# Four-stage MetaFormer: attention keys as the normed tokens, last tile centred by matmul, another late order, upper convolution rows by diagonal matmuls

## What is computed

```python
# stage 0, mixer: depthwise 3x3 convolution over 64 channels per image
xv, z = split(norm(x) @ in_proj_w.T)
xc = silu(depthwise_conv3x3(xv, conv_w, 'SAME') + conv_b)
# stage 2, feed-forward: 1024 serial steps over the pixels, 2 batches
yt = sigmoid(wx_t + yt @ V.T)
# stage 3, mixer; xn = (x - mean) / sqrt(var + eps) over the 32 channels
q, k, v = xn @ Wq, xn @ Wk, xn @ Wv          # 32 channels = 4 groups of 8, 2 heads of 4
# group 0: inside 8x8 windows, group 1: across them; group 2: inside 16x16, group 3: across
sim = einsum('id,jd->ij', q * 4 ** -0.5 ..., k) + pos   # the scale is DIM_HEAD ** -0.5
out = softmax(sim) @ v
x = x + concat(out_0..out_3) @ Wo + bo
```

## Time and profile before

| | us |
|---|---|
| median of 3 runs (lowest, highest) | 1099.59 (1097.26, 1099.84) |
| the profiled execution, its own time | 1096.21 |
| its span | 1094.3 |
| TensorE matmul busy | 735.8 (67%) |
| VectorE busy | 447.8 (41%) |
| ScalarE busy | 447.1 (41%) |
| POOL busy | 256.5 (23%) |
| recurrence's matmuls L835, 2048 records | 269.4 |
| its sigmoids L847, 1024 | 165.0 |

### The profile page before, as it was taken

The page is one execution under the profiler, slowest core; times in us unless marked ns, Lnnn a source line. Parts: engine busy times, 40 slices in busy tenths (PEclk is TensorE's granted clock), DMA queues, the critical chain, the costliest instruction groups (busy, mean ns, idle before and its releaser), DMA issues. The chain is left out here.

```text
span 1094.3 us, 11753 instructions
## 1 busy us (share of the span) xinstructions
PE 735.8 (67%) x4391; PEld 412.7 (38%) x4391; DVE 447.8 (41%) x746; ACT 447.1 (41%) x1473; POOL 256.5 (23%) x143
## 2 busy tenths in 40 slices
PE   7917888887886787655555555557887555685876
PEld 3302333333343443333333333334654333353543
DVE  5597999999956555400000000021152000220753
ACT  4454767676625543233333333332222333223532
POOL 3267989898810000200000000000000000000410
PEclk9966999999996588655555555555555555555887
DMA  3020000000000000200000000000000000000000
GB/s 67 2 58 0 1 0 1 0 1 0 1 1 5 1 22 9 63 1 1 1 1 0 1 1 1 1 1 0 1 1 1 1 1 0 1 1 1 1 22 11
DMA packets 9474, 7.64 MB, mean 7 GB/s; under 512 B 7154, under 2 KB 7970, under 8 KB 9128
## 3 DMA queue, kind: packets, MB, share of 16 engines
q1 hardware_dynamic: 9416, 6.88, 2.6%
HBM read 5.04 MB, written 0.26 MB: 5 GB/s over the span
## 5 line engine op out<-in xcount | busy, mean ns | idle before, releaser
L835 PE MATMUL L2p_z<-L2yx,L2v 64*32 64x2 f32 x2048 | 269.4, 199 | 230.5 <-ACT L2yx L847 225.5
L847 ACT ACTIVATE L2yx<-L2p_z 32x2 f32<-32x2 f32 x1024 | 165.0, 161 | 387.5 <-PE L2p_z L835 387.5
L835 PEld LDWEIGHTS L2p_z<-L2yx,L2v 64*32 64x32 f32 x2048 | 181.6, 136 | 336.3 <-ACT L2yx L847 316.6
L1486 DVE COPY xn<-L2yx 32x512 f32<-32x512 f32 (+2 forms) x3 | 1.0, 328 | 389.0 <-ACT L2yx L847 361.8
L621 POOL TENSOR_TENSOR hc<-hs,cb 128x1024 f32<-128x1024 f32 x64 | 149.4, 2355 | 20.6 <-DVE hs L604 20.5
L2100 POOL TENSOR_TENSOR prod<-e 128x1024 f32<-128x1024 f32 x2 | 3.8, 1932 | 558.5 <-DVE e L1614 558.5
L548 PE MATMUL p_y<-hc,ident 128*128 128x512 f32 x256 | 122.8, 602 | 5.0 <-DVE y_seq L587 2.8
L604 DVE TENSOR_TENSOR_SCAN hs<-d_a,p_bb 128x1024 f32<-128x1024 f32 x48 | 109.8, 2287 | 7.4 <-ACT d_a L571 1.4
L575 ACT ACTIVATE cb<-p_cb 128x1024 f32<-128x1024 f32 x64 | 65.0, 1016 | 7.0 <-PE p_cb L538 6.8
L548 PEld LDWEIGHTS p_y<-hc,ident 128*128 128x128 f32 x256 | 47.7, 191 | 50.0 <-issue 31.5
L571 ACT ACTIVATE d_a<-step,decay 128x1016 f32<-128x1016 f32 x48 | 54.6, 1138 | 23.7 <-DVE hs L604 23.1
(11 more groups left out here) (467 smaller groups left out, 942.5 us busy)
## 6 DMA issues: line engine op xcount, KB each, us to landing
y_seq<-in_pick SPq DMA_DIRECT2D x1, 768.0 KB
b_parts<-part SPq DMA_DIRECT2D x3, 256.0 KB, 3.7
c_parts<-part SPq DMA_DIRECT2D x3, 256.0 KB, 4.4
pos<-in_pos SPq DMA_DIRECT2D x1, 512.0 KB, 3.6
ao<-in_at_o SPq DMA_DIRECT2D x1, 512.0 KB, 3.8
L1w<-in_L_w SPq DMA_DIRECT2D x1, 297.0 KB
L3w<-in_L_w SPq DMA_DIRECT2D x1, 297.0 KB
x_tok<-in_x SPq DMA_DIRECT2D x2, 128.0 KB, 3.0
```

The costliest lines, as they stand in the source:

```text
L835: pe.matmul(p_z[0:C, t % 2, 0:NB], v[:, 0:C], yx[:, NB * t:NB * (t + 1)], start=True, stop=True).then_inc(s("preact"), 1)
L847: act.activation(yx[0:C, NB * (t + 1):NB * (t + 2)], p_z[0:C, t % 2, 0:NB], ACT.Sigmoid).then_inc(s("state"), 1)
```

## The change

1. **Convolution.** `acc` holds the lower 16 rows only; VectorE does all nine taps on them. For the upper 16, POOL multiplies the identity with each column of `w_conv` into nine 128 x 128 tables `taps` (in `step`), and TensorE sums the taps in PSUM: two strips of eight rows, nine matmuls of 256 columns each, in place of the 56 `keep_streaming` matmuls. ScalarE's three taps and POOL's additions go; the gates of the upper strips read PSUM.
2. **Keys.** q k^T = xn (Wq Wk^T) xn^T, so `aqk` = aq ak^T is made once (two matmuls and a copy), `q` is xo @ aqk, and `xo` itself, doubled to 128 partitions, is the key: `kk`, `copy_keys` and the key projections are gone. The tokens are turned back as 128 x 128 (`xn_two`).
3. **Last tile.** Two matmuls with a centring table (the second for the new states) and one that sums squares replace the turn, the norm by token and the turn back; POOL adds the last states to x. SP loads two more tensors, `centre` and `spread_var`.
4. **Order of the tail.** Another `RING`, other `late_banks`, units 9 and 11 shifted by ScalarE too, `scores1` and `finish1` split by head, the output of the groups across windows in two parts.

```diff
-                            keep_streaming(pe, norm.dump, 56)
+                            pe.wait_ge(sig["taps"], 1)
+                            pe.wait_ge(sig["padded_in"], 2)
+                            for wy in range(2):
+                                for k in range(9):
+                                    last = pe.matmul(p_a[:, wy * BANK:wy * BANK + WIN * SIDE], taps[:, k], tap_rows(k, WIN * wy, WIN), start=(k == 0), stop=(k == 8))
+                                last.then_inc(sig["conv_upper"], 1)
...
+                            for k in range(9):
+                                last = pool.tensor_scalar(taps[:, k], ident[:], w_conv[:, k:k + 1], None, ALU.mult)
...
-                            for k in range(1, 9 - AWAY):
-                                link(dve.scalar_tensor_tensor(acc[:], tap(k), w_conv[:, k:k + 1], acc[:], ALU.mult, ALU.add))
+                            for k in range(1, 8):
+                                link(dve.scalar_tensor_tensor(acc[:], tap_rows(k, MID, MID), w_conv[:, k:k + 1], acc[:], ALU.mult, ALU.add))
...
+                            gate(0, upper[0])
+                            act.wait_ge(sig["conv_lower"], 1)
+                            for wy in range(2):
+                                gate(2 + wy, acc[:, WIN * wy:WIN * wy + WIN])
+                            act.wait_ge(sig["conv_upper"], 2)
+                            gate(1, upper[1])
...
-        BY_ACT = (8, 10)
+        BY_ACT = (8, 9, 10, 11)
...
-                return pe.matmul(dst[:, 0:KEYS], q[rows, 0, t * 128:(t + 1) * 128], kk[rows, 0, k0:k0 + KEYS], start=True, stop=True)
+                return pe.matmul(dst[:, 0:KEYS], q[rows, 0, t * 128:(t + 1) * 128], xo[rows, 0, k0:k0 + KEYS], start=True, stop=True)
...
-                    ins = pe.transpose(self.p_back[0:R, t % 4 * 128:(t % 4 + 1) * 128], xn_tok[:, t], ident[:])
+                    ins = pe.transpose(self.p_back[:, t % 4 * 128:(t % 4 + 1) * 128], xn_two[:, t - a], ident[:])
...
+            def root_of(self, dve, link, minus_half, root, step):
+
+                link(dve.tensor_scalar(root.bitcast(I32), minus_half.bitcast(I32), -0.5, float(0x5f3759df - 2 ** 22 - 2 ** 30), ALU.mult, ALU.add))
                 for _ in range(3):
                     link(dve.tensor_tensor(step, root, root, ALU.mult))
-                    link(dve.tensor_tensor(step, step, half_var, ALU.mult))
+                    link(dve.tensor_tensor(step, step, minus_half, ALU.mult))
                     link(dve.scalar_tensor_tensor(root, step, 1.5, root, ALU.add, ALU.mult))
...
+            def centre_new(self, pe):
+                for b in range(NB):
+                    last = pe.matmul(self.p_tok[:, 0:128], centre[0:C, b], self.by_batch[0:C, T - 127:T + 1, b], start=False, stop=(b == NB - 1))
+                last.then_inc(sig["last_centred"], 1)
+
+            def sum_squares(self, pe):
+                pe.wait_ge(sig["squared"], 1)
+                pe.matmul(self.p_back[:, 0:128], spread_var[:], by_chan[:, 1], start=True, stop=True).then_inc(sig["last_centred"], 1)
...
+                for k in range(2):
+                    last = pe.matmul(p_q[:, 0, k * 128:(k + 1) * 128], aq[:, k], ak[:, k], start=True, stop=True)
+                    if k == 1:
+                        last.then_inc(sig["qk_made"], 1)
+                    yield
...
-                    for m, wgt in enumerate((aq, ak)):
-                        if made >= 2:
-                            pe.wait_ge(sig["qk_read"], made - 1)
-                        self.project(pe, 0, g, wgt, p_q[:, m])
-                        made += 1
-                        for _ in range(6):
-                            yield
+                    self.project(pe, 0, g, p_q[:, k])
+                    for _ in range(6):
+                        yield
...
-                late_banks = [p_q[:, 0], p_q[:, 1], p_tok[:], p_back[:]]
+                late_banks = [p_tok[:], p_back[:], p_q[:, 0], p_q[:, 1]]
...
-                RING = ["o0", "o1", "b0", "s14", "s15", "b1", "s16", "s17", "o2", "s18", "s19", "b2", "s20", "s21", "s22", "s23",
-                        "out", "o3", "b3"]
+                RING = ["o0", "s14", "s15", "b0", "o1", "s16", "s17", "b1", "s18", "s19", "o2", "s20", "s21", "b2", "s22", "s23",
+                        "x1", "o3", "x3", "b3"]
...
-                        self.add_states(dve, 2)
-                        self.norm(dve, link, 2)
+                        self.norm_last(dve, link)
...
                         biased(dve, late_banks, 8)
+                        scores1(0)
                         divide(0)
+                        biased(dve, late_banks, 9)
+                        scores1(1)
                         divide(1)
-                        scores1()
-                        biased(dve, late_banks, 9)
-                        shifted(dve, 9)
                         biased(dve, late_banks, 10)
```

More of the change, by code:

```diff
@@ L272, in _ @@
                             pool.memset(w_dt[:], 0.0)
[L273 to L277, removed]
+                            pool.wait_ge(sig["load_in"], 64)
+                            for k in range(9):
+                                last = pool.tensor_scalar(taps[:, k], ident[:], w_conv[:, k:k + 1], None, ALU.mult)
+                            last.then_inc(sig["taps"], 1)
                         @block.tensor
@@ new lines, in norm @@
+                self.root_of(dve, link, var, root, step)
+                root_twice = root.rearrange("p (g a c) -> p g a c", a=1, c=1).broadcast_to([128, n, 2, C])
+                dve.tensor_tensor(xn_two[:, 0:b - a].rearrange("p t (b d c) -> p (t b) d c", b=NB, d=2), twice_(tok), root_twice, ALU.mult).then_inc(sig["part_scaled"], 1)
+                dve.wait_ge(sig["part_back"], part + 1)
+                pixels = lambda side: self.p_back[:, a % 4 * 128:(a % 4 + b - a) * 128].rearrange("p (y v x) -> p v y x", v=SIDE // side, x=side)
@@ new lines, in norm @@
+                for g in self.ORDER[part]:
+                    side = 8 if g == 0 else 16
+                    for r, n, dst in strips(g, xo[:, WITHIN[g]], 4 * a, 4 * (b - a)):
+                        last = dve.tensor_copy(dst, pixels(side)[:, :, r:r + n])
+                    last.then_inc(sig["xo_made"], 1)
+            def root_of(self, dve, link, minus_half, root, step):
+                link(dve.tensor_scalar(root.bitcast(I32), minus_half.bitcast(I32), -0.5, float(0x5f3759df - 2 ** 22 - 2 ** 30), ALU.mult, ALU.add))
@@ L1603, in pieces @@
                         last = pe.matmul(p_1[b * 64:(b + 1) * 64, n * cols:(n + 1) * cols], window1(8 + 4 * part + n), ae1[:, b], start=True, stop=True)
-                    if n == 3:
+                    yield
+                cols = NB * 3 * HEADS * HC
+                for n in range(2):
+                    last = pe.matmul(p_3[:, n * cols:(n + 1) * cols], window3(part, 2 + n), ae3[:], start=True, stop=True)
+                    if n == 1:
                         last.then_inc(sig["e_made"], 1)
@@ L1658, in pe @@
                     yield
[L1659 removed]
+                pe.wait_ge(sig["qk_read"], 3)
                 pe.wait_ge(sig["e_read"], 1)
@@ L1700, in pe_bulk @@
                 yield from self.turn_scores(pe, FIRST)
+                for _ in range(6):
+                    yield
+                self.centre_old(pe)
             def pool(self, pool):
@@ L1856, in mix_across @@
                                 for b in range(NB):
-                                    last = pe.matmul(pixels[b * C:(b + 1) * C, w // 4 % 2, w % 4], ao[:, 1, w * C:(w + 1) * C], o_chan[:, 1, b * 64:(b + 1) * 64],
-                                                     start=False, stop=(w == 7))
-                                if w == 7:
-                                    last.then_inc(sig["at_across"], 1)
-                        keep_streaming(pe, p_o, 2)
-                        for _ in self.turn(pe, 2):
-                            pass
@@ L2183, in constants @@
         own_one[k, :, 2 * k:2 * k + 2] = 1.0
+    centre = np.zeros((NB, C, 2, NB, 2, C), np.float32)
+    for d in range(2):
+        for b in range(NB):
+            centre[b, :, 0, b, d] = np.eye(C) - 1.0 / C
+        centre[0, :, 1, 1, d] = np.eye(C) - 1.0 / C
+    spread_var = np.kron(np.eye(2 * NB), np.full((C, C), -0.5 / C)).astype(np.float32)
     return {
+        "centre": centre.reshape(NB * C, 2, 2 * NB * C),
+        "spread_var": spread_var,
         "ident": np.eye(128, dtype=np.float32),
```

412 lines of the change are left out of this document (219 added, 193 removed).

## The result

| | before | changed |
|---|---|---|
| median of 13 runs | 1097.26 | 1086.99 |
| lowest, highest | 1094.91, 1099.84 | 1084.41, 1094.83 |
| profiled execution, its time | 1096.21 | 1091.56 |
| its span | 1094.3 | 1089.6 |

The account below looks back on a forecast made before the run. TensorE is busy for most of every stretch, but the convolution's chain, the serial recurrence and the attention's tail hold the end. -5.0 - 4.3 - 1.9 = -11.2 takes the median 1099.59 to 1088.4, range 1081.5 to 1094.0.

Parts of the forecast that it names:

- Convolution, -5.0: Convolution block: with the taps split between VectorE and TensorE, the next stretch starts at 26.1 instead of 31.09.
- Rival C: Convolution: tables late at 0.85 each, so the block gives only -2.9 and the time is 1090.5; chance 0.15.
- Recurrence, -4.3: Recurrence's second half: four key projections go (-5.9), added products and half-centring +1.2, wider turns back +0.4.
- Rival E: Recurrence: the key projections were covered, giving 0 for -4.3 and a time of 1092.7; chance 0.05.
- Tail, -1.9: Attention's tail: -2.6 by laying out old and new orders, +0.7 for the clock; 49.4 instead of 51.3.
- the prediction's own signs of being wrong: A 256-column matmul over half a 512-column one, a falling convolution clock, or a tail longer than 51.3.
- The wait of turn(15): Tail: TensorE waits 4.1 us after turn(14) for the PSUM bank that divide(0) reads.
- So I let the first wait (4.1) halve the clock for some 3 us: +0.7: Tail: only TensorE's wait before turn(15) lowers the clock, for some 3 us, costing +0.7.
- -2.6 was forecast without the clock: Tail: laid out with the same durations, the old order ends at 1063.04, the new at 1060.45.
- Rival B: Tail: stays at half clock after the first wait, +5.5 for -1.9, time 1095.8; chance 0.07.
- Rival D: Tail: waits for the ring are shorter or leave the clock, -2.6 to -5.0, 1085.3 to 1087.7; chance 0.20.
- rival A: Convolution: without the 56 matmuls the clock falls to 0.5 there and in the next stretch, +6.1, 1105.7; chance 0.03.

Follow-up runs that it names:

- e1: The kernel before with only the convolution part of the change; median 1093.62, ratio to before 0.9964.
- e3: The changed kernel with divide(0) and divide(1) put ahead of scores1(0) and scores1(1) on VectorE; median 1079.31, ratio to before 0.9829.
- e4: The changed kernel with 14 matmuls without a result ahead of turn(15) and 6 ahead of turn(17); median 1086.64, ratio to before 0.9895.
- e5: The changed kernel with four more projections on TensorE, results unused, where keys were projected in the recurrence; one execution, 1099.89.
- e7: The changed kernel with divides 0, 1 and 2 moved ahead and four matmuls without a result before turn(15); median 1080.82, ratio to before 0.9833.
- e10: The changed kernel with divides 0, 1 and 2 moved ahead and two TensorE gaps in the tail's start filled; median 1077.99, ratio to before 0.9836.
- e8: The changed kernel with one 128-column bf16 matmul without a result behind each step of the recurrence's first half; time 1086.95.
- e9: The changed kernel with divide(0), divide(1) and divide(2) moved ahead on VectorE, no added matmuls; median 1080.70, ratio to before 0.9844.
- e2: The changed kernel with the convolution of before, so keys, last tile and tail order alone; median 1094.78, ratio to before 0.9966.
- e11: The changed kernel with nine more 128-element scalings on POOL ahead of the nine tables, making them late; one execution, 1099.48.

## Why the prediction was right, and where it was off

- **Convolution, -5.0: right.** The next block starts at 26.62 in the changed kernel's trace and at 26.06 to 26.39 in those of e1, e3, e4, e5, e7 and e10, forecast 26.1; at 27.24 in e8 and 31.75 in e9 (last section). Tables: 0.60 each for 0.53, hidden as said, by 0.7. The gates and the clock were as forecast; VectorE's half ended 0.8 later (23.7 for 22.9) and still ahead of TensorE's. Rival C fell with the 0.60. At the start of the recurrence e1 has 3.9 of its 4.9 left.
- **Recurrence, -4.3: right.** -4.00 in the changed kernel, e2, e3, e4, e7 and e8, 3.85 and 3.11 in e9 and e10, and e5 gives the term of the four projections alone, 5.89 for 5.9. The added work is 1.9 for 1.6; the trace has 0.474 for a turn back, as forecast. Rival E fell.
- **Tail, -1.9: wrong, +0.7 in the pair of traces and +2.0 in the mean of five.** A tail longer than before was one of the prediction's own signs of being wrong. Its first term, -2.5 at the first bias, was -2.4. The wait of turn(15) was 3.68 for 4.1. The step that failed is "So I let the first wait (4.1) halve the clock for some 3 us: +0.7". The fall lasted 6.8 us, there was a second one of 6.8 behind the wait for divide(1), and together they cost 4.1 (e4; 3.0 to 4.4 by the other traces), not 0.7. With them VectorE's waits for scores came to 8.9 where 4.9 was laid out. I had read the length from a window of mine, 1042 to 1045, that lay within a longer stretch; the slices of 1 us of the same trace have 0.50 until 1048, and again from 1055 to 1058, which I did not look at. The rest of the laying out was good: with the start at its 14.74 and e4's rest of 33.68 the tail would take 48.42, 3.4 under the old one, where -2.6 was forecast without the clock; the 4.1 of the clock makes it +0.7.
- **Rival B** (half clock to the end) did not happen: from 1038.40 to 1056.33 the granted clock is 1.00, transposes or not. The Trainium skill, "TensorE: Matmul & The Clock Gate", Part 4, would have transposes not count as activity; no stretch of only transposes is in these traces, so this is not tested, but with values and mixes among them the clock came back both times. **Rival D** did not happen with this order; e3 shows that it was to be had.
- **The sum.** Forecast -11.2, measured -10.3 (7.5 to 11.6 by the interval). The tail was 2.6 worse than forecast, so 8.6 is what the right steps leave: inside the interval. The last 1.7 of the median's difference are not assigned to a stage, and by the mean tail of the five traces it would be 3.0. Stages that the change leaves alone scatter: from the first matmul of stage 1's feed-forward to the next stage 23.99 to 26.63 in thirteen traces, from the last one's gate projection to the output 18.22 to 21.45. That the sum came within 0.9 of the measured difference, with one of its three terms of the wrong sign, is luck. One figure of the range is off by a little: 1085.3 - 3.4 - 0.18 is 1081.7, not 1081.5.

## What to carry to other kernels

When an operation of one engine frees a buffer for another, put it ahead of any long work that nobody waits for: here swapping `divide` and `scores1`, equal work in another order, was worth 7.7 us by the medians, beside the 10.3 of the whole change. Price a wait of TensorE with the clock behind it (here some 4 us for two waits), and read how long the clock stays down from narrow slices over the whole stretch, not from the window that first shows it. And where work is moved to TensorE to take it from the end of a block, its clock is on the path from then on: a late input costs its lateness and the slower matmuls behind it (6.4 and 2.8 in e11).

## What the runs showed of the hardware that was not expected

- TensorE's records covered 242 of 258 us in e8, with a granted clock of 0.50 all through, while in the convolution and in most of the tail it stood at 1.00. Filling the gaps with small matmuls did not raise it. Which property of the work the clock follows stays open here; only the 128-column filler was tried.
- The same start of the tail took 14.74 (five traces), 16.8 (three) or 18.3 to 18.5 (two), by what the clock did in it. In the five it rose 6.5 to 7.4 us after the recurrence's last matmul and stayed up (at 1008.8 in e3); in the three it rose after 5.9 to 6.5 us and fell again for 6.8 (in e4 from 1011.6 to 1018.4); in the two it rose after some 18 us only (at 1020.9 in e7). What decides between these is not shown: but for e10's fillers the instructions of the start are the same.
- In e9's trace the matmuls of the convolution block took twice as long up to 24.94, and the next block started at 31.75:

```profile
13.82 3.78 PE L286 MATMUL p_v<-xn,w_in 64*128 64x512 f32 x4
17.39 3.62 PE L287 MATMUL p_z<-xn,w_in 64*128 64x512 f32 x4
20.94 10.00 PE L294 MATMUL p_a<-padded,step 128*128 128x256 f32 x36
...
20.94:24.94 4.00, 4.00 (x10) 3.19 (x10) 3.82 (x6) 2.31 (x2) 0.00 (x0) 1.00 0.00 0
24.94:30.50 5.56, 5.56 (x27) 4.88 (x26) 0.20 (x1) 1.27 (x3) 0.00 (x0) 1.00 0.00 0
```

The projection `p_z` took 3.62 for 1.88 in the changed kernel's trace, and a record of a diagonal matmul 0.43 up to 24.94 and 0.215 after it, though both windows show 1.00. The reason is in the trace's list of clock levels. It has no entry before 24.94 in e9, and a window counts time without an entry as 1.00. In the other twelve traces the first entry, a rise to 1.00, stands between 11.5 and 14.5, and the durations turn with it: in e1 a norm matmul's record takes 0.42 up to 12.9 and 0.27 after it. So the first 1.00 of a trace is to be read from durations, and in e9 the clock was at its lower level until 24.94. That is near what rival A feared, at 0.03, though not by a fall: the rise came late, in one of ten traces with the new convolution, and puts that block's end 0.66 behind the old one's. This execution took 1086.76, e9's other four 1077.69 to 1081.54. Why the rise came so late is not shown; TensorE had been at work without a gap from 13.8 to 24.9. It may be part of the spread of the changed kernel's runs, 1084.41 to 1094.83. How the old convolution fares with a late rise no trace shows.
